# First attention of a four-stage network: passes batch by batch, V for four heads at once, loops written out

## What is computed

```python
q = jnp.einsum('bsd,hed->bhse', x, W_Q)
k = jnp.einsum('bsd,hed->bhse', x, W_K)
v = jnp.einsum('bsd,hed->bhse', x, W_V)
scores = jnp.einsum('bhse,bhme->bhsm', q, k) * scale
scores = jnp.where(causal, jnp.float32(-1000000000.0), scores)
pattern = jax.nn.softmax(scores, axis=-1)
z = jnp.einsum('bhsm,bhme->bhse', pattern, v)
out = jnp.einsum('bhse,hde->bsd', z, W_O)
x = _layernorm(x + out)
```

## Time and profile before

| | |
|---|---|
| runs of the kernel, us | 2424.32, 2425.41, 2425.58 (median 2425.41) |
| profiled execution, span from first to last instruction, us | 2423.6 |
| its own whole time | not given beside the span |
| mean granted TensorE clock | 0.955 |
| instructions | 36462 |
| first attention | from the start to about 990 us |

### The profile page before, as it was taken

How to read it: one execution, slowest core, us unless ns; L and a number is a source line. 1 busy time by engine, 2 the same in 40 slices (tenths; PEclk the granted TensorE clock), 3 DMA queues, 4 the chain that set the end, 5 groups by cost and what they waited for, 6 DMA issues and landing times. The chain is left out here.

```text
span 2423.6 us, 36462 instructions
## 1 busy us (share of the span) xinstructions
PE 2238.1 (92%) x11264; PEld 1719.0 (71%) x11264; DVE 1561.5 (64%) x2879; ACT 1196.9 (49%) x2397; POOL 567.5 (23%) x550
## 2 busy tenths in 40 slices
PE   6999999999999999679999669999998689999996
PEld 5888888888888888558788434554543458877885
DVE  4666666666666666646566558887882436655665
ACT  4555555555555555344334316666666334433442
POOL 2333333333333333112222210000000012222221
PEclk9999999999999999879999869999999769999998
DMA  2000000000000000011111061212210011111111
GB/s 66 16 17 16 15 16 16 16 15 15 15 15 15 15 9 1 1 38 46 46 46 46 9 145 24 30 27 37 31 26 12 1 38 46 48 50 39 46 49 47
DMA packets 45297, 73.19 MB, mean 30 GB/s; under 512 B 6651, under 2 KB 21798, under 8 KB 44710
## 3 DMA queue, kind: packets, MB, share of 16 engines
q1 hardware_dynamic: 44710, 72.10, 12.2%
q10 hardware_dynamic: 512, 0.13, 0.0%
HBM read 64.74 MB, written 7.34 MB: 30 GB/s over the span
## 5 line engine op out<-in xcount | busy, mean ns | idle before, releaser
L1399 POOL TENSOR_TENSOR a_pr<-a_pr,a_rinv 128x128 f32<-128x128 f32 (+7 forms) x256 | 294.0, 1149 | 598.0 <-DVE a_rinv L1636 598.0
L1068 DVE TENSOR_REDUCE a1m_part<-psum 128x1 f32<-128x512 f32 x512 | 320.8, 683 | 93.4 <-PE psum L914 92.8
L1040 ACT ACTIVATE a1m_pt<-psum 128x512 f32<-128x512 f32 x512 | 265.6, 604 | 115.7 <-PE psum L934 107.6
L647 DVE SCALAR_TENSOR_TENSOR f_hid<-psum,f_bias_now,f_act_s 128x512 f32<-128x512 f32 x168 | 126.0, 750 | 267.0 <-ACT f_act_s L604 196.9
L504 POOL TENSOR_TENSOR f_lo_gu<-f_raw_gu,f_hi_gu 128x512 fp32r<-128x512 f32 x84 | 109.1, 1298 | 783.2 <-ACT f_hi_gu L579 783.2
L604 ACT ACTIVATE f_act_s<-psum,f_bias_now 128x512 f32<-128x512 f32 x168 | 115.7, 689 | 337.4 <-PE psum L71 263.8
L1563 ACT ACTIVATE a_pth<-psum 128x512 fp32r<-128x512 f32 (+3 forms) x384 | 174.6, 490 | 193.6 <-PE psum L1455 192.6
L69 PE MATMUL psum<-xh,f_hi_gu 128*128 128x512 f32 x672 | 265.9, 396 | 2.0 <-POOL f_lo_gu L504 1.3
L71 PE MATMUL psum<-xh,f_lo_gu 128*128 128x512 f32 x672 | 264.3, 393 | 0.0
L70 PE MATMUL psum<-xl,f_hi_gu 128*128 128x512 f32 x672 | 263.6, 392 | 0.0
L914 PE MATMUL psum<-a_ks,a_qm 128*128 128x512 f32 x512 | 224.2, 452 | 23.6 <-DMA a_qm<-a_qd 20.9
(11 more groups left out here) (225 smaller groups left out, 4937.4 us busy)
## 6 DMA issues: line engine op xcount, KB each, us to landing
f_raw_gu<-in_gu SPq DMA_DIRECT2D x84, 256.0 KB, 2.7
a_wr<-in_qkv SPq DMA_DIRECT2D x32, 384.0 KB, 3.1
f_raw_dn<-in_down SPq DMA_DIRECT2D x84, 128.0 KB, 2.0
a_qm<-a_qd SPq DMA_DIRECT2D x48, 128.0 KB, 5.3
a_qt<-a_qd SPq DMA_DIRECT2D x48, 128.0 KB, 3.9
yT<-in_xT SPq DMA_DIRECT2D x4, 512.0 KB, 6.1
a_wor<-in_o SPq DMA_DIRECT2D x16, 128.0 KB, 2.0
a_qd<-a1p_hi SPq DMA_DIRECT2D x2, 1024.0 KB, 14.0
```

The costliest lines, as they stand in the source:

```text
L1040: act.activation(pt[:, kp % 2, g, k, :], st_ps[:, bank(place(c, kp, g, k)), :], ACT.Exp, scale=1.0 / HD1).then_inc(exp_done, 1)
L1068: dve.tensor_reduce(part[:, c, q, g, half:half + 1], mx_ps[:, bank(at + g * 2 + half), :], AX.X, ALU.max).then_inc(mx_taken, 1)
L1399: pool.tensor_tensor(pr[:, j, 0:n], pr[:, j, 0:n], rinv[:, j:j + 1].to_broadcast([P, n]), ALU.mult).then_inc(p_done, 1)
```

## The change

- The passes run batch by batch: pass hb is sequence hb // 16, head hb % 16.
- V is projected for four heads at once, with 128 tokens stationary and the four heads' 512 columns moving. It comes out with tokens on partitions, so the copy and the transposes go. The eight tasks ("v", 0) to ("v", 7) of a group stand in units 2 to 7 of its leading pass (hb % 4 == 0), for that pass and the three after it.
- q1 moves from unit 3 to unit 2 and k1 from unit 4 to unit 3. Units 4 and 5 hold tasks in leading passes alone.
- `prepare` goes. Its loads, rounding and splitting are in the attention's block: chunks 0 and 1 ahead of the first tasks, chunks 2 and 3 in units 4 and 5 of pass 0, and the weights of pass 0 are loaded first. `PRE` has q and k alone.
- The weights of q and k are split in two steps, both behind normalise(5); the output weights are loaded, rounded (unit 4) and split (unit 5) in every pass; V's four matrices (1024 columns) are rounded in unit 4 and split in unit 5 of passes 2, 6, ..., 26, for the group that begins two passes later.
- zh, zl, which had two slots, have one. Each probability buffer is a tile of its own.
- All loops are written out and semaphore targets are constants.

The core of the diff:

```diff
-    PLAN = [[("pv", 1, True)],
-            [("q", 0), ("k", 0)],
-            [("o", 1, True, 0)],
-            [("o", 1, True, 1), ("q", 1)],
-            [("k", 1), ("vt", 0)],
-            [("vt", 1), ("v", 0)],
-            [("pv", 0, False), ("v", 1)],
-            [("o", 0, False, 0), ("o", 0, False, 1)]]
...
-    PRE = [("q", 0), ("k", 0), ("q", 1), ("k", 1), ("vt", 0), ("vt", 1), ("v", 0), ("v", 1)]
...
+    def plan(hb):
+        first, last, lead = hb == 0, hb == HB - 1, hb % VG == 0
+        units = [[] if first else [("pv", 1, True)],
+                 [] if last else [("q", 0), ("k", 0)],
+                 ([] if first else [("o", 1, True, 0)]) + ([] if last else [("q", 1)]),
+                 ([] if first else [("o", 1, True, 1)]) + ([] if last else [("k", 1)]),
+                 [], [],
+                 [("pv", 0, False)],
+                 [("o", 0, False, 0), ("o", 0, False, 1)]]
+        if lead:
+            for t, qt in enumerate((2, 3, 4, 4, 5, 5, 6, 7)):
+                units[qt].append(("v", t))
+        if last:
+            units.append([("pv", 1, False), ("o", 1, False, 0), ("o", 1, False, 1)])
+        return units
+    PRE = [("q", 0), ("k", 0), ("q", 1), ("k", 1)]
+    WHOLE = ("o",)
...
+        wr = ph.sb("wr", [P, 2, 2, DT, E0])
+        wh = ph.sb("wh", [P, 2, 2, DT, E0], F32R)
+        wl = ph.sb("wl", [P, 2, 2, DT, E0], F32R)
+        wvr = ph.sb("wvr", [P, DT, VG, E0])
+        wvh = ph.sb("wvh", [P, DT, VG * E0], F32R)
+        wvl = ph.sb("wvl", [P, DT, VG * E0], F32R)
...
-            with eng.Fori(0, H0 - 2) as h:
-                half(h * 2 + 1, h, 1, False, False)
-                half(h * 2 + 2, h + 1, 0, False, False)
-            half(HB - 3, H0 - 2, 1, False, False)
-            half(HB - 2, H0 - 1, 0, False, False)
-            half(HB - 1, H0 - 1, 1, False, True)
...
+            def load(n):
+                if n >= 2:
+                    sp.wait_ge(wl_done, (n - 1) * 2)
+                sp.dma_start(wr[:, n % 2], a["qkv0"][n % H0, :, 0:2]).then_inc(wr_in[n % 2], 16)
+            def load_v(g):
+                if g >= 1:
+                    sp.wait_ge(wvl_done, g)
+                h0 = g * VG % H0
+                for h in range(VG):
+                    sp.dma_start(wvr[:, :, h, :], a["qkv0"][h0 + h, :, 2]).then_inc(wv_in, 16)
+            def load_o(n):
+                if n >= 1:
+                    sp.wait_ge(wol_done, n)
+                sp.dma_start(wor[:], a["o0"][n % H0]).then_inc(wor_in, 16)
+            load(0)
+            load_x(0)
+            load_x(1)
+            load_v(0)
+            load(1)
             load_o(0)
-            with sp.Fori(1, H0) as h:
-                load(h * 2, 0, h)
-                load(h * 2 + 1, 1, h)
-                load_o(h)
+            load_x(2)
+            load_x(3)
+            for hb in range(HB):
+                if hb + 2 < HB:
+                    load(hb + 2)
+                if hb + 1 < HB:
+                    load_o(hb + 1)
+                if hb % VG == 0 and hb + VG < HB:
+                    load_v(hb // VG + 1)
...
+            split(0)
+            split_v(0)
+            normalise(0, 0)
+            split(1)
+            split_o(0)
+            for hb in range(HB):
+                    if after(hb, qt + 1)[0] < HB:
+                        normalise(*after(hb, qt + 1))
+                    if qt == 4 and hb + 2 < HB:
+                        split(hb + 2)
+                    if qt == 5 and hb >= 1:
+                        split_o(hb)
+                    if qt == 5 and hb % VG == 2 and hb + 2 < HB:
+                        split_v(hb // VG + 1)
...
+                elif kind == "v":
+                    if c == 0:
+                        pe.wait_ge(wvl_done, hb // VG + 1)
+                    x0 = hb // H0 * S + c * P
+                    for dt in range(DT):
+                        i = mm3(pe, o, xh[:, dt, x0:x0 + P], xl[:, dt, x0:x0 + P], wvh[:, dt, :], wvl[:, dt, :],
...
+                    if n % VG == 0:
+                        pe.wait_ge(task_out, PLACE[n, ("v", CQ * (c + 1) - 1)] + 1)
+                    v0 = n % VG * E0
...
+            pe.wait_ge(ident_done, 1)
+            for t in PRE:
+                task((-1, t))
+            pe.wait_ge(rounded, 2)
+            for qt in range(2):
+                scores(0, qt)
+            for hb in range(HB):
+                for qt, tasks in enumerate(PLANS[hb]):
+                    if qt < NQ:
+                        if after(hb, qt + 2)[0] < HB:
+                            scores(*after(hb, qt + 2))
+                        turn(hb, qt)
                     for t in tasks:
...
+                        task((hb, t))
...
+            round_weights(0)
+            round_x(0)
+            round_x(1)
+            for t in PRE[:2]:
+                task((-1, t))
+            act.wait_ge(mask_set, 1)
+            act.activation(mask[:], mask0[:], ACT.Copy).then_inc(rounded, 1)
+            act.activation(idr[:], ident[:], ACT.Copy).then_inc(rounded, 1)
+            for t in PRE[2:]:
+                task((-1, t))
+            round_v(0)
+            for qt in range(2):
+                soften(0, qt)
+            round_weights(1)
+            round_o(0)
+            for hb in range(HB):
+                for qt, tasks in enumerate(PLANS[hb]):
+                    if qt < NQ:
+                        keep_hi(hb, qt)
+                        if after(hb, qt + 2)[0] < HB:
+                            soften(*after(hb, qt + 2))
                     for t in tasks:
                         if t[0] not in WHOLE:
...
+                            task((hb, t))
+                    if hb == 0 and qt in (4, 5):
+                        round_x(qt - 2)
+                    if qt == 3 and hb + 2 < HB:
+                        round_weights(hb + 2)
+                    if qt == 4 and hb >= 1:
+                        round_o(hb)
+                    if qt == 4 and hb % VG == 2 and hb + 2 < HB:
+                        round_v(hb // VG + 1)
...
+            keep_x(0)
+            keep_x(1)
+            for t in PRE:
+                task((-1, t))
+            for qt in range(2):
+                maximum(0, qt)
+            invert(0, 0)
+            for hb in range(HB):
+                for qt, tasks in enumerate(PLANS[hb]):
+                    if qt < NQ:
+                        if after(hb, qt + 1)[0] < HB:
+                            invert(*after(hb, qt + 1))
+                        if after(hb, qt + 2)[0] < HB:
+                            maximum(*after(hb, qt + 2))
+                        keep_lo(hb, qt)
+                    if hb == 0 and qt in (4, 5):
+                        keep_x(qt - 2)
                     for t in tasks:
...
+                        task((hb, t))
...
-        prepare(nc, "in", a["xT"], xh, xl, yT, ident)
```

More of the change, by code:

```diff
@@ L1263, in causal_attention @@
+    PRE = [("q", 0), ("k", 0), ("q", 1), ("k", 1)]
+    WHOLE = ("o",)
+    PLANS = [plan(hb) for hb in range(HB)]
+    FLAT = [[(-1, t) for t in PRE]] + [[(hb, t) for unit in PLANS[hb] for t in unit] for hb in range(HB)]
+    PLACE = {key: k for k, key in enumerate(key for row in FLAT for key in row)}
+    HIS = {}
+    for key in PLACE:
+        if key[1][0] not in WHOLE:
+            HIS[key] = len(HIS)
     NB = CQ + 2 * (NQ - CQ)
@@ L1402, in half @@
-            def half(hb, h, b, first, last):
-                for qt in range(NQ):
-                    if qt < NQ - 1:
-                        normalise(hb, qt + 1)
-                    elif not last:
-                        normalise(hb + 1, 0)
-                    if SPLITS <= qt < SPLITS + 3 and (not isinstance(hb, int) or hb < HB - 2):
-                        split(hb + 2, b, qt - SPLITS)
-                    if qt == NQ - 3 and b == 0 and not first:
-                        split_o(h)
@@ L1498, in task @@
-                i.then_inc(task_done, 1)
-            def half(hb, h, b, first, last):
-                k, n = bases(hb)[0], 0
-                for qt, tasks in enumerate(plan(first, last)):
-                    if qt < NQ - 2:
-                        scores(hb, b, qt + 2)
-                    elif not last:
-                        scores(hb + 1, 1 - b, qt + 2 - NQ)
-                    turn(hb, qt)
-                    for t in tasks:
-                        task(hb, h, b, t, k + n, bank_of(b, first, n))
-                        n += 1
@@ L1512, in begin @@
-            def begin():
-                pe.wait_ge(rounded, 2)
-                for n, t in enumerate(PRE):
-                    task(-1, 0, 1, t, n, n % 2)
-                for qt in range(2):
-                    scores(0, 0, qt)
-            def end():
-                k = bases(HB - 1)[0] + sum(len(u) for u in plan(False, True))
-                for n, t in enumerate([("pv", 1, True), ("o", 1, True, 0), ("o", 1, True, 1)]):
-                    if t[0] == "o" and t[3] == 0:
-                        pe.wait_ge(task_out, k + 1)
-                    finish(t, k + n)
```

(18 more changed lines are left out.)

370 lines of the change are left out of this document (126 added, 244 removed).

## The result

The changed kernel takes 2465.26 us (median of 4 runs, 2463.86 to 2468.74), the kernel before 2425.49 (4 runs, 2424.32 to 2427.80): ratio 1.0166 [1.0151, 1.0180], **39.8 us slower**. The profiled spans are 2462.7 and 2423.6, 39.1 apart.

The account below looks back on a forecast made before the run. TensorE's work was taken as the bound, busy 92% of the span. Terms −23.8 − 10.8 + 1.4 + 1 + 50.1 + 13 + 3 + 15 = +49 us on 2425.4 gave 2474 us; range 2432 to 2495.

Parts of the forecast that it names:

- V (−23.8): TensorE's V work: 113.6 us of projections and transposes removed, 89.8 us of grouped projections added; net −23.8 us.
- The pause (+50.1): TensorE waits before tile 6's transposes for GpSimd's normalisation, units 4 and 5 being bare: 2.2 us in 22 passes, +50.1 us.
- My lower value of 1.55: Lower size of the pause before tile 6's transposes, from the earlier kernel's last pass: 1.55 us each, total +35.7 us.
- GpSimd's V split (+13): In passes 2, 6, ..., 26 it stands ahead of normalising tile 7, so TensorE waits: +1.9 us, 7 times, +13.
- V's eighth task (+3): After a leading pass the late pv1 waits for this task's tile: 8 × 0.4 = +3 us, 0 to 8.
- The start (−10.8 + 1.4 + 1): First matmul at 8.9 us, −10.8; GpSimd's first V split and rounding, +1.4; later input chunks rounded in pass 0, +1.
- The loops (0): Writing out the loops changes nothing, since passes in and out of the loop are equally busy: 0, −2 to +2 us.
- The clock (+15): Clock falls after the new pauses before tile 6's transposes: 10 of 30 pauses at 1.5 us, +15 us, bounds 0 and 50.
- my first rival (2459): Same pauses before tile 6's transposes, but the clock stays up: 2459 us, chance 0.25.

Follow-up runs that it names:

- e7: Changed kernel; non-leading passes: q1 in unit 4, k1 in unit 5; V's eighth task in unit 6; V's rounding and split in the pass before leading ones: 2406.57 us.
- e8: e7 with the two q and k weight splits moved behind the normalisations of tile 7 and of the next pass's first tile: 2404.79 us.
- e12: Changed kernel with q1 in unit 4 and k1 in unit 5 of passes that lead no group, nothing else: 2422.14 us.
- e2: Changed kernel with the two q and k weight splits moved from behind tile 5 to behind tile 7 and the next pass's first tile: 2453.35 us.
- e3: Changed kernel with GpSimd's split of V's matrices moved from unit 5 to unit 1 of the pass after, just before the leading one: 2461.13 us.
- e4: Changed kernel with V's eighth task moved from unit 7 to unit 6 of the leading passes: 2452.08 us.
- e5: Changed kernel with the input's loads, rounding and splitting put back in a block of their own ahead of the attention: 2469.01 us.
- e9: Changed kernel with the third and fourth input chunks rounded and kept in unit 1 of passes 2 and 3 instead of in pass 0: 2468.03 us.
- e6: Kernel before with the two hardware loops of its attention written out, nothing else: 2426.59 us, ratio 0.9998.
- e10: e8 with the third and fourth input chunks moved to passes 2 and 3, as in e9: 2408.62 us.

## Why the prediction was right, and where it was off

**The total.** Forecast 2474, measured 2465.3: inside the range, slower as forecast, 8.8 us too high. Without the clock's term its sum was +33.9 up to the mark, and the mark moved by 34.1. That is closer than its terms were, and so far luck: the pause and V's split came out 7 to 10 and 2 us smaller than their terms, the start and the eighth task cost 5 and 9 to 10 us more, and these errors cancelled. The clock's term of 15 is what made the forecast too high.

**V (−23.8).** Confirmed within some 4 us. Per group, from the working's prices, it is 8 × 1.38 + 0.18 − 4 × 3.55 = −3.0 us. With nearly all waits removed (e7, e8) a group is 118.40 against 120.87, −2.5. Its passes that don't lead take 26.8 us from one late pv1 to the next; 30.22 − 3.55 would be 26.67. So the parts of the change that no run takes apart (the order by batch, the single slot of zh and zl, the output weights in every pass) cost some 0.1 us a pass there.

**The pause (+50.1).** Mechanism shown, by e12 above all. Size: 43.1 us by its removal, 1.71 a pass for a forecast of 2.2. GpSimd is last in 16 of the 23 passes, as forecast (1.60 us, in pass 30 only 1.17). In the other seven the pause of 1.71 ends with VectorE's low half of tile 5, late behind the rounding of V's matrices on ScalarE, which has no term in the sum; e2 shows this wait by itself. In the row of pass 7 the chain is 6.22 us for 6.41, and the work beside it 6.22 − 1.61 − 0.18 = 4.43 for 4.21: the two small errors are the difference. My lower value of 1.55 was nearer to it.

**GpSimd's V split (+13).** Mechanism shown by e3's waits, 10 us, 1.50 each for a forecast of 1.9; in time the clock took most of that back there.

**V's eighth task (+3).** This is the step of the sum that was mis-sized: 13.2 us by e4 (1.49 a group, 11.9, by the groups without a spell). The leading passes show it too, 39.5 us for a forecast of 38, and in e7 and e8, where this wait is gone, 38.0. I priced it as one wait, for the tile of the task before. I did not follow the bank: the eighth task itself has to wait for the output projection whose bank it takes. The prediction gave 0 to 8 for it, and it lies outside.

**The start (−10.8 + 1.4 + 1).** The first matmul is at 8.72 (forecast 8.9), V's split took 2.36 (2.41), and e5's mark of pass 0 against e9's, 56.9 − 48.7 = 8.2 (up to 1.7 of it the clock's, 6.8 against 3.4 us at 1.2 GHz), is a little under 9.4. The later chunks in pass 0 cost 4.5 instead of 1, beyond the 0 to 3 that I allowed, so the whole is worth 3.7. What I had not followed are the 4.0 us of waits (1.42 and 2.59) that TensorE has there for V's tiles.

**The loops (0).** Shown by e6.

**The tally** of one group, from single experiments: V −3.0, pause 3 × 1.71 = 5.1, V's split 1.6, eighth task 1.5: +5.2 us, and the trace has 126.02 − 120.87 = +5.15.

**The clock (+15).** Wrong in place. Up to the mark TensorE was at 1.2 GHz for 13.7 us, before for 3.4, so at most 5 us more, where the sum had 15; and of the 22 pauses in steady passes that wait for GpSimd and the 7 that wait for a_ptl only one was followed by a spell (at 366.9). For these pauses my first rival (2459) was nearly right. The Trainium skill (TensorE: Matmul & The Clock Gate, Why this matters for your kernels) warns only of idle gaps longer than any of these, and 28 of the 29 agree with it. The one at 366.9, and those of e3 and e9 with spells right behind idle times of 1.71 and 2.07 us, do not; the measurement decides.

**What stays open: +5 us in unchanged code.** Behind the mark the instructions are the same, and the half-clock time there is 214.8 us before and 235.6 after; 21 us at half speed are worth up to 10. Among the profiles of the experiments it is 225 to 243, and that part takes 1440.1 to 1446.3 us; e6, whose first attention is that of the kernel before, has 1442.1, in an execution that was 3 us longer than its median. So single executions differ by some us there. But the two profiles that are compared lie within 1 us of the medians of their kernels (span + 1.8: 2425.4 and 2464.5), so the 5 us are not just an unlucky pair. Why the clock is lower there, no run shows.

## What to carry over

Before moving work off a unit, ask what it covers. A chain through four engines (scores, maximum, exponential, reciprocal, normalisation, turn) does not get shorter with the work beside it, here 6.2 us, and independent matmuls have to stand there; tasks put beside it lengthen it, to 7.1 us, when their own steps stand in the same queues. 23.8 us of saved work turned into 39.8 us of loss. With two projections a pass moved back under the chain the kernel was level with the one before, and with V's eighth task and V's rounding and split moved too the saving became a gain of 20 us. When a task is put into a rotation of two banks, follow the bank as well as the data. And work moved out of a place where it costs 4.5 us needs a place with slack on VectorE, or it costs more there.

## What was unexpected of the hardware

- **Spells at 1.2 GHz are not tied to a length of idleness one to one.** 28 of 29 pauses of 1.2 to 1.7 us in steady passes of the changed kernel had none behind them; e3, with fewer pauses, had five in the same part. In the profiles of all these kernels together, one execution each, none of 73 pauses of 1.0 to 1.2 us in steady passes had a spell right behind it, 14 of 146 of 1.5 to 1.7 us had one, and three of four of 2.07 us (two each in e9 and e10).
- **What a removed wait gives can be taken back by the clock.** In e3, 10 us less waiting moved the mark by 1.5 us, with 17 us more at half clock.
